# Linear attention: the second query round and the last value copies moved across the copy of the turned key maxima

## The chip, the cores and the metric

The kernel runs on one core of a Trainium2 chip. The metric is the device time of one execution in microseconds, as the median of three runs. The engines are named as in the profile: PE (TensorE), DVE (VectorE), ACT (ScalarE), POOL (GpSimd) and SP (the DMA queue used here). Each engine takes its own instructions in order; engines wait for each other through semaphores.

## What is computed

The program is a chain of seven layers on an input of 32 images of 32 channels and 16 x 16 pixels: a group norm and a linear attention, a convolution with a shared 51 x 51 kernel, a linear transformer, a mixture of experts, a squared attention and routed blocks. The change touches only the first layer, whose reference is, cut to what matters:

```
qkv = einsum('bchw,oc->bohw', xn, w_qkv)      # xn: x scaled to unit norm over channels
q, k, v = split(qkv, 3, axis=1)               # 4 heads of 32 channels, n = 256 pixels
k = concatenate([mk, k], axis=-1)             # 4 memory columns ahead of the pixels
v = concatenate([mv, v], axis=-1)
q = softmax(q, axis=-2) * scale               # over the 32 channels of a head
k = softmax(k, axis=-1)                       # over the pixels
context = einsum('bhdn,bhen->bhde', k, v)
out = einsum('bhde,bhdn->bhen', context, q)
return einsum('bchw,oc->bohw', out, w_out) + b_out
```

## The kernel before

The images lie on the partitions in four groups of 32 channels (J = 4), and the pixels of eight images per group are cut into 16 units of 128 tokens. `linear_attention` projects them in four rounds of four units for each of queries, keys and values. A query round takes PSUM banks 0 to 3, a value round and a key round take banks 4 to 7. Each engine's order is written out by hand; nothing is scheduled by a planner, and the only freedom that an engine has is to wait.

What each engine does in the stretch that the change touches:

- PE: query_round(0), value_round(2), value_round(3); then a transpose of the key maxima in parts (L484, into bank 4), a transpose of the memory exponentials (L487, bank 5) and a small memory product (L490, bank 6), each waiting for what the engine ahead copied; then key_round(0), query_round(1), key_round(1), key_round(2), query_round(2), key_round(3) and the context products (L456), between which the turned queries (L445) and query_round(3) stand. A query round waits until the units of the round ahead have been subtracted (they share the banks), a key round until ACT has taken the exponentials of the key round ahead.
- DVE: for every unit a `subtract_maxima` (L573 the maximum of each head, L575 the subtraction out of PSUM into SBUF) and an `invert_sums` (L581 the sum of the exponentials, L583 its reciprocal). In round 0, behind unit 2, it copies the turned key maxima (L599), the turned memory exponentials (L601) and the memory product (L603) out of PSUM. Behind the last unit of a round stand the four `invert_sums` of that round.
- ACT: four value copies for each value round (L646: four banks, 512 columns a unit), the factors of the memory terms (L668), then query exponentials (L657) and pairs of key exponentials (L651) in a fixed order: queries 0 to 3, keys 0, keys 1, queries 4 to 6, keys 2, query 7, keys 3, query 8, and then query exponentials between copies of the turned queries (L661).
- POOL: key maxima in three parts, the memory terms (they wait for L603 on DVE), and for every unit the product of the exponentials with their inverted sums (L760).

The transpose of the key maxima writes bank 4, which the last value round has filled, so it waits until all value units are copied. The copy L599 gives the rows that open each key product, so key_round(0) waits for it and for L603.

Of the kernel before, what the change touches and what calls it, by code (L numbers as in the profile page):

```python
# [9 lines left out]
ACT = mybir.ActivationFunctionType  # L10
# [3 lines left out]
B, C, H, W = 32, 32, 16, 16  # L14
# [5 lines left out]
NCH = COLS // CH  # L20
QN = 4
NQ = N // QN
HEADS, DH = 4, 32
# [247 lines left out]
def linear_attention(nc, m, sem, d):  # L271

    ps = m.ps
    UN = G * S
    RND = 4
# [29 lines left out]
    memterm = sem("la_memterm")  # L305
    v_ready = sem("la_v_ready")
    v_copied = sem("la_v_copied")
    k_ready = sem("la_k_ready")
    kexp_done = sem("la_kexp_done")
    q_ready = sem("la_q_ready")  # L310
# [48 lines left out]
    def qf_unit(u):  # L359

        g, s = divmod(u, S)
        return qf[:, :, :].rearrange("p (j g) n -> p j g n", j=J)[:, :, g, s * 128:(s + 1) * 128]

    def turned_queries(u):
        return ps[:, 7 - u % 2, :].rearrange("p (j n) -> p j n", j=J)
# [7 lines left out]
    with nc.Block() as block:  # L373
        @block.tensor
        def _(pe):
# [26 lines left out]
            def value_round(r):  # L402

                if r:
                    pe.wait_ge(v_copied, RND * r)
                for i in range(RND):
                    for j in range(J):
                        mm = pe.matmul(ps[:, 4 + j, i * 128:(i + 1) * 128], xn[rows_of(j), tokens(RND * r + i)],
                                       m.wvo[rows_of(j), :], start=True, stop=True)
                mm.then_inc(v_ready, 1)  # L410
# [16 lines left out]
            def query_round(r):  # L427

                if r:
                    pe.wait_ge(qsub_done, RND * r)  # L430
                for i in range(RND):
                    for j in range(J):
                        mm = pe.matmul(ps[:, j, i * 128:(i + 1) * 128], xn[rows_of(j), tokens(RND * r + i)],
                                       m.wqkv[rows_of(j), 0:128], start=True, stop=True)
                mm.then_inc(q_ready, 1)
# [26 lines left out]
            def key_maxima_round(r):  # L462

                for i in range(J):
# [14 lines left out]
            query_round(0)  # L479
            value_round(2)  # L480
            value_round(3)
            pe.wait_ge(parts, 4)
            pe.wait_ge(v_copied, UN)
            pe.transpose(ps[:, 4, 0:64].bitcast(BF16), m.kparts[:, :, :].rearrange("p j r -> p (j r)"),  # L484
                         m.identb[:, :]).then_inc(turned, 1)
            pe.wait_ge(memexp_done, 1)
# [6 lines left out]
            pe.wait_ge(turned_copied, 1)  # L493
            pe.wait_ge(w2mem_copied, 1)
            key_round(0)
            query_round(1)
            key_round(1)
            key_round(2)
            query_round(2)
# [27 lines left out]
        def _(dve):  # L527
            own = sem("la_dve")
            for g in range(G):
                c = slice(g * N, (g + 1) * N)  # L530
# [3 lines left out]
            for g in range(BY_ACT, G):  # L534
                c = slice(g * N, (g + 1) * N)
# [53 lines left out]
                                  m.kmem[:, b0:b1, :], ALU.add).then_inc(w2_summed, 1)  # L589

            for r in range(NCH):
                dve.wait_ge(q_ready, r + 1)
                for i in range(RND):
                    subtract_maxima(RND * r + i)
                    if r == NCH - 1 and i:
                        invert_sums(RND * r + i - 1)
                    if r == 0 and i == 2:
                        dve.wait_ge(turned, 1)
                        dve.tensor_copy(m.kmrow[:, :], ps[:, 4, 0:64].bitcast(BF16)).then_inc(turned_copied, 1)  # L599
                        dve.wait_ge(mem_ready, 1)  # L600
                        dve.tensor_copy(m.kemt[:, :], ps[0:MEM, 5, 0:128]).then_inc(mem_copied, 1)  # L601
                        dve.wait_ge(w2mem_ready, 1)
                        dve.tensor_copy(m.w2mem[:, :], ps[:, 6, 0:33]).then_inc(w2mem_copied, 1)  # L603
                    if r == 2 and i == 2:
                        dve.wait_ge(memterm, 2)
                        sum_context(0)
                for i in range(RND if r < NCH - 1 else 0):
                    invert_sums(RND * r + i)
# [24 lines left out]
        @block.scalar  # L633
        def _(act):
            for g in range(BY_ACT):
                c = slice(g * N, (g + 1) * N)
                act.activation(m.tmpB[:, c], m.x[:, c], ACT.Square, bias=m.shift8[:, g:g + 1],
                               scale=m.inv8[:, g:g + 1]).then_inc(squared, 1)
            act.wait_ge(norm2_ready, 1)
            act.activation(m.rstd[:, NQ:2 * NQ], ps[:, 4, 0:NQ], ACT.Sqrt).then_inc(norm_ready, 1)  # L640
            act.wait_ge(memmax_ready, 1)
            act.activation(m.kem[:, :], m.memk[:, :], ACT.Exp, bias=m.small[:, 1:2]).then_inc(memexp_done, 1)

            def copy_values(u):
                i = u % RND
                act.activation(m.vtok1[u][:, :, :, 0:C],  # L646
                               ps[:, 4:8, i * 128:(i + 1) * 128].rearrange("p j (h c) -> p j h c", h=HEADS),
                               ACT.Copy).then_inc(v_copied, 1)

            def key_exponentials(r, a):  # L650
                act.activation(ek[:, RND * r:RND * (r + 1), 2 * a:2 * a + 2, :].rearrange("p u j d -> p j u d"),  # L651
                               ps[:, 4 + 2 * a:6 + 2 * a, :].rearrange("p j (u d) -> p j u d", u=RND),
                               ACT.Exp).then_inc(kexp_done, 1)

            def query_exponentials(u):
                act.wait_ge(qsub_done, u + 1)
                act.activation(qt[:, u, :, :], qt[:, u, :, :], ACT.Exp).then_inc(qexp_done, 1)  # L657

            def copy_queries(u):
                act.wait_ge(qt_ready, u + 1)  # L660
                act.activation(qf_unit(u), turned_queries(u), ACT.Copy).then_inc(qt_copied, 1)  # L661

            for r in range(NCH):
                act.wait_ge(v_ready, r + 1)
                for i in range(RND):
                    copy_values(RND * r + i)
            act.wait_ge(km_ready, 1)
            act.activation(m.kfac[:, :], m.kmax[:, :], ACT.Exp, bias=m.small[:, 0:1], scale=-1.0).then_inc(f_done, 1)  # L668
            def key_round(r):
                act.wait_ge(k_ready, r + 1)  # L670
                for a in range(2):
                    key_exponentials(r, a)

            for u in range(RND):
                query_exponentials(u)
            key_round(0)
            key_round(1)
            for u in (4, 5, 6):
                query_exponentials(u)
            key_round(2)  # L680
            query_exponentials(7)
            key_round(3)
            query_exponentials(8)
            copy_queries(0)
            query_exponentials(9)
            query_exponentials(10)
            copy_queries(1)
            query_exponentials(11)
            copy_queries(2)
            for i in range(4):  # L690
                query_exponentials(12 + i)
                copy_queries(3 + i)
            for u in range(7, UN):
                if u not in BY_V:
                    copy_queries(u)
# [2270 lines left out]
```

## Time and profile before

| what | before |
|---|---|
| median of three runs | 572.55 us (572.53 to 574.28) |
| profiled execution | 572.74 us |
| its span, first to last instruction | 570.9 us |
| mean granted TensorE clock | 0.956 of full speed |
| PE busy | 503.4 us, 88% of the span |
| DVE busy | 409.6 us, 72% |
| ACT busy | 311.7 us, 55% |
| POOL busy | 158.4 us, 28% |

The profile is one execution. Times in it are in microseconds from the start of the span, durations of single instructions in nanoseconds. 1.84 us lie outside the span. An engine's busy time does not say whether it is waited for: the timeline shows each instruction with its start, its duration and, in brackets, the idle time ahead of it with the instruction that ended it. The linear attention runs from about 10 to 86 us of the span.

### The profile page before, as it was taken

To read this page: it belongs to the slowest core of one execution; us is meant where nothing else is said; L and a number is where in the kernel's file an instruction comes from. 1 tells how busy PE (TensorE), PEld (TensorE's weight loads), DVE (VectorE), ACT (ScalarE), POOL (GpSimd) and SP (SyncE) were. 2 spreads that over 40 slices of the span, in tenths; PEclk is the share of its full clock that TensorE was granted. 3 is DMA by queue.
4 is the path that set the end of the run, shared out by engine and by line. 5 is a ranking of instruction groups with operands and counts; after the bars stand their busy time and mean duration, and the time that the engine had idled before them with its cause. 6 is when DMAs were issued, how large, how long until landed. Compare 5 with 4: busy or idle time off the path is not lost. (4 is left out here: it accounts for less than half of the span.)

```text
span 570.9 us, 15184 instructions
## 1 busy us (share of the span) xinstructions
PE 503.4 (88%) x6313; PEld 293.7 (51%) x6313; DVE 409.6 (72%) x751; ACT 311.7 (55%) x543; POOL 158.4 (28%) x210
## 2 busy tenths in 40 slices
PE   8957778999888889989888878989999999999993
PEld 3547654466665553255555544444664566366520
DVE  5758978686444589967788857975786776777664
ACT  3255635243344310267988875355776577667573
POOL 0106423000000000043565640000692078038600
PEclk9976899999999879999999999979999999999998
DMA  8400007000000075000000000000000000000002
GB/s 262 47 6 3 3 2 242 1 2 1 2 1 2 1 175 121 0 3 1 2 1 2 3 20 2 0 8 13 1 3 6 8 2 1 12 2 2 1 7 77
DMA packets 22560, 15.02 MB, mean 26 GB/s; under 512 B 17466, under 2 KB 20570, under 8 KB 22363
## 3 DMA queue, kind: packets, MB, share of 16 engines
q1 hardware_dynamic: 22490, 14.00, 9.8%
q8 instruction: 55, 0.90, 0.6%
q14 instruction: 15, 0.11, 0.1%
HBM read 8.71 MB, written 1.08 MB: 17 GB/s over the span
## 5 line engine op out<-in xcount | busy, mean ns | idle before, releaser
L2327 DVE TENSOR_REDUCE R<-ps 128x4 f32<-128x1024 f32 x48 | 56.6, 1221 | 21.3 <-PE ps L1849 20.9
L2150 ACT ACTIVATE R<-ps 128x512 f32<-128x512 f32 x96 | 52.0, 597 | 11.0 <-PE ps L1861 10.9
L2233 POOL TENSOR_TENSOR R<-R 128x512 f32<-128x512 f32 x42 | 53.3, 1270 | 16.4 <-ACT R L2150 16.4
L1609 POOL TENSOR_TENSOR R<-R 128x512 f32<-128x512 f32 x32 | 45.4, 1417 | 39.8 <-DVE R L1542 39.8
L1542 DVE TENSOR_TENSOR R<-ps,lasting 128x512 f32<-128x512 f32 x64 | 41.1, 685 | 11.7 <-PE ps L1464 11.7
L1861 PE MATMUL ps<-tmpA,R 32*128 32x256 f32 x384 | 48.3, 378 | 0.0
L1576 ACT ACTIVATE R<-R 128x1536 f32<-128x1536 f32 x32 | 47.3, 1479 | 0.1
L1849 PE MATMUL ps<-R,tmpA 32*128 32x256 f32 x384 | 45.4, 392 | 0.0
L1464 PE MATMUL ps<-R,Q 32*128 32x128 f32 (+1 forms) x512 | 29.9, 346 | 10.0 <-ACT R L1592 10.0
L1861 PEld LDWEIGHTS ps<-tmpA,R 32*128 32x128 f32 x384 | 36.5, 185 | 0.5
L1464 PEld LDWEIGHTS ps<-R,Q 32*128 32x128 f32 x512 | 23.9, 184 | 20.8 <-DVE R L1542 16.9
L2008 PE MATMUL ps<-R,early 32*128 32x512 f32 x160 | 31.2, 713 | 1.2 <-DVE R L166 1.2
L1849 PEld LDWEIGHTS ps<-R,tmpA 32*128 32x128 f32 x384 | 29.6, 184 | 4.0 <-ACT tmpA L2124 2.3
L2217 POOL TENSOR_TENSOR R<-R 128x8 f32<-128x8 f32 x24 | 4.9, 206 | 94.9 <-DVE R L2327 94.9
L2173 ACT ACTIVATE R<-ps,b 128x1024 f32<-128x1024 f32 x25 | 26.8, 1113 | 7.1 <-PE ps L2008 7.1
L1592 ACT ACTIVATE R<-ps 128x256 f32<-128x256 f32 x64 | 24.2, 381 | 10.1 <-DVE R L1542 10.1
L101 PE MATMUL ps<-lasting 128*128 128x512 f32 x54 | 28.9, 664 | 0.6 <-DVE R L1124 0.6
L1492 PE MATMUL ps<-R 128*32 128x128 f32 (+1 forms) x512 | 27.2, 332 | 2.1 <-ACT R L1576 2.1
L2390 DVE TENSOR_SCALAR R<-ps,b 128x1024 f32<-128x1024 f32 x15 | 19.3, 1284 | 9.8 <-PE ps L2008 9.1
L1910 PE MATMUL ps<-R,Q 128*32 128x256 f32 x384 | 25.6, 384 | 0.0
L2062 PE MATMUL ps<-R,early 128*32 128x512 f32 x160 | 22.4, 631 | 1.2 <-DVE R L2390 1.2
L1108 DVE COPY R<-ps 32x256 f32<-32x256 f32 (+2 forms) x30 | 14.0, 477 | 11.5 <-PE ps L1042 3.9
(336 smaller groups left out, 1103.9 us busy)
## 6 DMA issues: line engine op xcount, KB each, us to landing
R<-z SPq DMA_DIRECT2D x32, 128.0 KB, 2.4
R<-in_qv SPq DMA_DIRECT2D x1, 2560.0 KB
x<-in_x SPq DMA_DIRECT2D x4, 256.0 KB, 3.5
out<-x SPq DMA_DIRECT2D x4, 256.0 KB, 2.6
lasting<-in_lasting SPq DMA_DIRECT2D x1, 811.0 KB, 8.4
early<-in_early SPq DMA_DIRECT2D x1, 793.5 KB, 7.0
scatter<-in_scatter SPq DMA_DIRECT2D x1, 512.0 KB, 5.4
P<-scratch_w SPq DMA_DIRECT2D x16, 32.0 KB, 2.6
```

The source lines that it names most:

```text
L101: pe.matmul(m.ps[:, bank, :], t[:, 0:128], t[:, 0:CH], start=True, stop=True)
L1464: mm = pe.matmul(ps[:, 2 * (u % 3) + k, s * N:N + s * 128], k_[rows, at:at + 128], m.qm[rows, h, at:(g + 1) * N], start=True, stop=True)
L1492: mm = pe.matmul(ps[rows_of(j), 6 + g % 2, s * 128:N], vm[:, (2 * g + s) * J + j, h, :], m.att[:, u % SLOTS, k, at:at + N - s * 128], star ...
L1542: dve.tensor_tensor(diagonal(u), ps[:, 2 * (u % 3):2 * (u % 3) + 2, :] .rearrange("p k (d n) -> p k d n", n=128)[:, :, 0:3:2, :], m.causal ...
L1576: act.activation(a, a, ACT.Silu, scale=1.0 / AHD).then_inc(act_done, 1)
L1609: pool.tensor_tensor(diagonal(u), diagonal(u), diagonal(u), ALU.mult).then_inc(diag_squared[1], 1)
L1849: return pe.matmul(ps[:, j, half * N:(half + 1) * N], ut[rows_of(j), at:at + 128], h[rows_of(j), cols], start=True, stop=True)
L1861: mm = pe.matmul(ps[:, turned_bank(g, j), t * N:(t + 1) * N], h[rows_of(j), at:at + 128], ut[rows_of(j), g * N:(g + 1) * N], start=False, ...
L2008: mm = pe.matmul(ps[:, 2 * (r % 3) + i, :], m.w1[p][rows_of(j), :], h[rows_of(j), k * CH:(k + 1) * CH], start=True, stop=True)
L2150: act.activation(m.et[:, g % 2, j, :], ps[:, turned_bank(g, j), :], ACT.Exp)\
L2233: pool.tensor_tensor(m.esum[:, g % 2, two, :], m.et[:, g % 2, two, 0:N], m.et[:, g % 2, two, N:2 * N], ALU.add).then_inc(sg["halves_added" ...
L2327: dve.tensor_reduce(m.parts[:, g % 2, :, a:a + 2, 3 * g].rearrange("p s i -> p i s"), ps[:, a:a + 2, :].rearrange("p i (s m) -> p i s m", ...
```

## The change

Three things move or are split.

- query_round(1) stands on PE right behind value_round(3), ahead of the transpose of the key maxima, instead of behind key_round(0).
- The four value copies of the last round are split by banks: ACT copies banks 4 and 5 of each unit (256 columns), DVE banks 6 and 7 (another 256). The transpose of the key maxima waits for both, through a second semaphore.
- On DVE the three copies of the turned parts stand behind unit 3 instead of unit 2 of round 0, and around them: the four value copies and the subtraction of unit 4 ahead, the subtractions of units 5, 6 and 7 behind. The four sums of round 0 come behind those, and round 1 of the loop is left with its sums alone.

```diff
--- before.py
+++ after.py
@@ -305,6 +305,7 @@
     memterm = sem("la_memterm")
     v_ready = sem("la_v_ready")
     v_copied = sem("la_v_copied")
+    v_copied_v = sem("la_v_copied_v")
     k_ready = sem("la_k_ready")
     kexp_done = sem("la_kexp_done")
     q_ready = sem("la_q_ready")
@@ -360,6 +361,13 @@
 
         g, s = divmod(u, S)
         return qf[:, :, :].rearrange("p (j g) n -> p j g n", j=J)[:, :, g, s * 128:(s + 1) * 128]
+
+    def value_unit(u, j0):
+        return m.vtok1[u][:, j0:j0 + 2, :, 0:C]
+
+    def value_banks(u, j0):
+        i = u % RND
+        return ps[:, 4 + j0:6 + j0, i * 128:(i + 1) * 128].rearrange("p j (h c) -> p j h c", h=HEADS)
 
     def turned_queries(u):
         return ps[:, 7 - u % 2, :].rearrange("p (j n) -> p j n", j=J)
@@ -479,8 +487,10 @@
             query_round(0)
             value_round(2)
             value_round(3)
+            query_round(1)
             pe.wait_ge(parts, 4)
             pe.wait_ge(v_copied, UN)
+            pe.wait_ge(v_copied_v, RND)
             pe.transpose(ps[:, 4, 0:64].bitcast(BF16), m.kparts[:, :, :].rearrange("p j r -> p (j r)"),
                          m.identb[:, :]).then_inc(turned, 1)
             pe.wait_ge(memexp_done, 1)
@@ -493,7 +503,6 @@
             pe.wait_ge(turned_copied, 1)
             pe.wait_ge(w2mem_copied, 1)
             key_round(0)
-            query_round(1)
             key_round(1)
             key_round(2)
             query_round(2)
@@ -589,18 +598,27 @@
                                   m.kmem[:, b0:b1, :], ALU.add).then_inc(w2_summed, 1)
 
             for r in range(NCH):
-                dve.wait_ge(q_ready, r + 1)
+                if r != 1:
+                    dve.wait_ge(q_ready, r + 1)
                 for i in range(RND):
-                    subtract_maxima(RND * r + i)
+                    if r != 1:
+                        subtract_maxima(RND * r + i)
                     if r == NCH - 1 and i:
                         invert_sums(RND * r + i - 1)
-                    if r == 0 and i == 2:
+                    if r == 0 and i == RND - 1:
+                        for u in range(UN - RND, UN):
+                            dve.wait_ge(v_ready, NCH)
+                            dve.tensor_copy(value_unit(u, 2), value_banks(u, 2)).then_inc(v_copied_v, 1)
+                        dve.wait_ge(q_ready, 2)
+                        subtract_maxima(RND)
                         dve.wait_ge(turned, 1)
                         dve.tensor_copy(m.kmrow[:, :], ps[:, 4, 0:64].bitcast(BF16)).then_inc(turned_copied, 1)
                         dve.wait_ge(mem_ready, 1)
                         dve.tensor_copy(m.kemt[:, :], ps[0:MEM, 5, 0:128]).then_inc(mem_copied, 1)
                         dve.wait_ge(w2mem_ready, 1)
                         dve.tensor_copy(m.w2mem[:, :], ps[:, 6, 0:33]).then_inc(w2mem_copied, 1)
+                        for u in range(RND + 1, 2 * RND):
+                            subtract_maxima(u)
                     if r == 2 and i == 2:
                         dve.wait_ge(memterm, 2)
                         sum_context(0)
@@ -660,10 +678,13 @@
                 act.wait_ge(qt_ready, u + 1)
                 act.activation(qf_unit(u), turned_queries(u), ACT.Copy).then_inc(qt_copied, 1)
 
-            for r in range(NCH):
+            for r in range(NCH - 1):
                 act.wait_ge(v_ready, r + 1)
                 for i in range(RND):
                     copy_values(RND * r + i)
+            act.wait_ge(v_ready, NCH)
+            for u in range(UN - RND, UN):
+                act.activation(value_unit(u, 0), value_banks(u, 0), ACT.Copy).then_inc(v_copied, 1)
             act.wait_ge(km_ready, 1)
             act.activation(m.kfac[:, :], m.kmax[:, :], ACT.Exp, bias=m.small[:, 0:1], scale=-1.0).then_inc(f_done, 1)
             def key_round(r):
```

On PE, from query_round(0) to the first key products of the stretch: L433 is a query round, L408 two value rounds, L484, L487 and L490 the turned parts, L420 and L423 the products of a key round. Before:

```order
L433 MATMUL ps<-early,tmpA 128x128 x16
L408 MATMUL ps<-P,tmpA 128x128 x32
L484 MATMUL ps<-identb,P 128x128
L487 MATMUL ps<-lasting,P 4x128
L490 MATMUL ps<-P 32x33 x4
L420 MATMUL ps<-P 128x128 x4
```

And now, with the new line numbers:

```order
L441 MATMUL ps<-early,tmpA 128x128 x16
L416 MATMUL ps<-P,tmpA 128x128 x32
L441 MATMUL ps<-early,tmpA 128x128 x16
L494 MATMUL ps<-identb,P 128x128
L497 MATMUL ps<-lasting,P 4x128
L500 MATMUL ps<-P 32x33 x4
L428 MATMUL ps<-P 128x128 x4
```

A second query round has come in between the value rounds and the transposes; its old place behind the first key round is empty.

On DVE, from the subtraction of unit 2 on: L573 and L575 are a unit's maximum and subtraction, L599, L601 and L603 the copies of the turned parts, L581 and L583 a sum and its reciprocal. Before:

```order
L573 TENSOR_REDUCE z<-ps 128x16
L575 TENSOR_TENSOR R<-ps,z 128x512
L599 COPY P<-ps 128x128
L601 COPY P<-ps 4x128
L603 COPY P<-ps 128x33
L573 TENSOR_REDUCE z<-ps 128x16
L575 TENSOR_TENSOR R<-ps,z 128x512
L581 TENSOR_REDUCE z<-R 128x16
```

And now, from the subtraction of unit 3 on:

```order
L582 TENSOR_REDUCE z<-ps 128x16
L584 TENSOR_TENSOR R<-ps,z 128x512
L611 COPY R<-ps 128x8x32 x3
L611 COPY P<-ps 128x8x32
L582 TENSOR_REDUCE z<-ps 128x16
L584 TENSOR_TENSOR R<-ps,z 128x512
L615 COPY P<-ps 128x128
L617 COPY P<-ps 4x128
L619 COPY P<-ps 128x33
```

Ahead of the copies of the turned parts stand now the subtraction of unit 3, four value copies and the subtraction of unit 4; behind them three more units and only then the sums.

## Rows read from the trace of the kernel before

**Rows 1.** Stretches, length, busy PE, PEld, DVE, ACT, POOL (instructions), granted clock, DMA.

```profile
36.50:38.50 2.00, 2.00 (x32) 1.72 (x32) 0.09 (x1) 0.00 (x0) 0.00 (x0) 0.50 0.00 0
38.60:42.30 3.70, 0.81 (x10) 0.31 (x10) 0.75 (x4) 3.70 (x8) 0.00 (x0) 0.50 0.02 4
42.40:46.40 4.00, 4.00 (x77) 3.86 (x80) 3.86 (x9) 1.84 (x3) 4.00 (x4) 0.50 0.01 2
46.60:49.80 3.20, 1.63 (x54) 1.33 (x48) 3.10 (x7) 1.56 (x3) 1.98 (x2) 1.00 0.02 5
50.80:55.30 4.50, 4.42 (x80) 3.94 (x80) 3.78 (x9) 3.17 (x5) 2.17 (x3) 0.50 0.01 2
...
60.20:63.40 3.20, 3.20 (x84) 2.47 (x84) 3.10 (x8) 1.63 (x3) 0.02 (x1) 0.50 0.02 5
63.60:68.80 5.20, 5.17 (x260) 4.32 (x249) 5.03 (x11) 3.01 (x6) 3.84 (x4) 1.00 0.02 3
56.10:74.90 18.80, 14.52 (x611) 11.90 (x611) 18.22 (x36) 10.36 (x18) 8.55 (x10) 0.89 0.02 4
```

**Rows 2.** Timeline, value round to key round: start, us, engine, line; idle in brackets.

```profile
33.25 0.69 DVE L575 TENSOR_TENSOR R<-ps,z 128x512 f32<-128x512 f32 x1
...
34.57 0.69 DVE L575 TENSOR_TENSOR R<-ps,z 128x512 f32<-128x512 f32 x1
...
36.42 2.09 PE L408 MATMUL ps<-P,tmpA 32*128 32x128 f32 x32 [2.19 <-ACT R L646]
...
38.58 1.57 ACT L646 ACTIVATE R<-ps 128x512 f32<-128x512 f32 x3 [2.21 <-PE ps L408]
...
40.03 0.62 ACT L646 ACTIVATE P<-ps 128x512 f32<-128x512 f32 x1
...
40.79 0.26 PE L484 MATMUL ps<-identb,P 128*128 128x128 bf16 x1 [2.28 <-ACT P L646]
...
41.09 0.23 DVE L599 COPY P<-ps 128x128 bf16<-128x128 bf16 x1 [4.50 <-PE ps L484]
...
42.38 0.29 PE L420 MATMUL ps<-P 32*128 32x128 bf16 x4 [0.41 <-DVE P L603]
```

**Rows 3.** Groups by line and form, copies out of PSUM: busy us, mean ns.

```profile
L1108 DVE COPY R<-ps 32x256 f32<-32x256 f32 x18 | 7.7, 426 | 4.3 <-PE ps L1042 3.9
...
L613 DVE COPY R<-ps 128x512 f32<-128x512 f32 x3 | 2.1, 687 | 2.6 <-PE ps L445 2.6
...
L910 ACT ACTIVATE R<-ps 128x256 f32<-128x256 f32 x8 | 3.1, 386 | 11.4 <-PE ps L877 11.4
```

**Rows 4.** Timeline of the key rounds, up to the copies of turned queries.

```profile
44.90 1.81 PE L433 MATMUL ps<-early,tmpA 32*128 32x128 f32 x32
...
45.19 1.94 ACT L651 ACTIVATE R<-ps 128x1024 f32<-128x1024 f32 x2 [0.97 <-PE ps L423]
...
47.19 0.23 PE L420 MATMUL ps<-P 32*128 32x128 bf16 x4 [0.47 <-ACT R L651]
...
48.77 1.94 ACT L651 ACTIVATE R<-ps 128x1024 f32<-128x1024 f32 x2 [1.64 <-PE ps L423]
...
53.30 1.92 PE L433 MATMUL ps<-early,tmpA 32*128 32x128 f32 x32
...
53.59 1.94 ACT L651 ACTIVATE R<-ps 128x1024 f32<-128x1024 f32 x2 [1.33 <-PE ps L423]
...
56.08 0.69 DVE L581 TENSOR_REDUCE z<-R 128x16 f32<-128x512 f32 x1 [1.36 <-ACT R L657]
...
57.69 1.94 ACT L651 ACTIVATE R<-ps 128x1024 f32<-128x1024 f32 x2 [1.64 <-PE ps L423]
...
59.77 0.24 PE L456 MATMUL ps<-R 128*32 128x33 f32 x5 [2.17 <-ACT R L651]
...
77.68 0.69 DVE L613 COPY R<-ps 128x512 f32<-128x512 f32 x1 [1.77 <-PE ps L445]
```

**Rows 5.** Busy time by stretch, a later stage.

```profile
340.10:343.30 3.20, 3.20 (x5) 1.22 (x4) 0.00 (x0) 1.11 (x2) 0.14 (x1) 0.50 0.31 84
```

## The prediction

> **What bounds the kernel now.** I read the page's slices first: ahead of 60 us no engine is full for long and the granted TensorE clock dips below one, so this stage is bound by hand-overs and not by one engine. Then I read the timeline from the last value round to the first context products, and last the busy times by stretch, for the clock. Two things are to be seen.
>
> First, a hand-over around 38 to 42 us. The last value round ends on PE at 36.42 + 2.09 = 38.51; ACT copies its four units from 38.58 to 40.65; only then may PE transpose the key maxima (40.79), DVE copy them (41.09) and, behind it, the memory terms, and PE begin key_round(0) at 42.38 [rows 2]. DVE stands for 4.50 us in front of the copy at 41.09 [rows 2].
>
> Second, a ring behind it: key_round(r) on PE writes four banks, ACT takes their exponentials, and only then may key_round(r+1) write the same banks. ACT's four pairs of exponentials start at 45.19, 48.77, 53.59 and 57.69, and the first context product stands at 59.77 [rows 4]. The steps are 3.58, 4.82, 4.10 and 2.08 us, and each is PE's round, then ACT's 1.94. The step of 3.58 has its key round at a granted clock of 1.00 (2.4 GHz), the step of 4.82 at 0.50 (1.2 GHz) [rows 1]: 1.24 us is what a key round costs more at the low level. query_round(1), which the change takes out of this ring, runs at 44.90 to 46.71, under ACT's 45.19 to 47.13 [rows 4]: it costs the ring nothing. DVE is nearly full after that, but its own start there hangs on the ring: at 56.08 it has waited 1.36 us for ACT, which issues query exponential 7 behind the third pair of key exponentials [rows 4].
>
> **The change, part by part.**
>
> Query round 1 behind the last value round. It waits for the subtraction of unit 3, now also ahead on DVE: a unit takes 1.32 us from start to start (33.25 to 34.57) [rows 2], so the third ends at 33.25 + 2 x 1.32 + 0.69 = 36.6 and unit 3 at 37.9, before the value round does. No wait. The round costs PE 1.81 to 1.92 us at the low level [rows 4], overlapping the tail of what is ahead of it by 0.2, so it ends near 40.2, and the transpose queued behind it can start there.
>
> Value copies on two engines. Four copies of 256 columns on ACT cost at most 4 x 0.386 = 1.54 us, end by 40.1. The trace has no DVE copy of 128 x 256; the nearest are 32 x 256 at 0.426 us and half of a 512-column one at 0.687 [rows 3]: four lie between 4 x 0.34 = 1.37 and 4 x 0.43 = 1.70. I take 1.6, nearer to the row with the same column count; from 38.58 they end at 40.2 (39.95 to 40.3), against 40.65 before. So the transpose stands at about 40.3 instead of 40.79: 0.5 us earlier. No work on DVE hides the four copies, but they lie in its 4.50 us wait.
>
> The subtraction of unit 4 in front of the copy of the key maxima. DVE is in order, and this pair waits for query round 1 (40.2) and takes 1.32 us. The transposed maxima are ready at 40.6 and lie there: DVE gets to them at about 41.6 instead of 41.09. Queued behind that pair are the two memory copies, PE's memory product, all key rounds, and POOL's memory terms. The chain from the copy to key_round(0), 41.09 to 42.38, keeps its 1.29 us. So key_round(0) starts near 42.9: **+0.5 us**. The bounds are +0.35 (copies at 1.37 and the query round at its overlap) and +0.7 (query round without overlap, 40.4).
>
> Subtractions 5 to 7 move ahead of the sums of round 0. ACT waited for unit 3 ahead of its fourth query exponential and no longer does, but that lies inside its wait for key_round(0): nothing. DVE's work behind the hand-over is two subtractions shorter, 2.64 us, and starts 0.5 later, so it is 2.1 us ahead at the end of round 1. The wait of 1.36 us at 56.08 only grows by that, because query exponential 7 stays queued on ACT behind the third pair of key exponentials: nothing. POOL's normalising of units 0 to 3 starts about 3 us later, since DVE's sums of round 0 now stand behind subtractions 5 to 7 instead of one; it is 4 us of work [rows 1] and its first taker stands behind 59.77 [rows 4]: nothing.
>
> The clock. Before, the rise to 1.00 came at the end of 4 us in which PE was full, key_round(0) and query_round(1) back to back (42.40 to 46.40 busy 4.00, granted 0.50), and key_round(1) then ran at 1.00 (46.60 to 49.80) [rows 1]. The change takes query_round(1) out of that place: behind key_round(0) PE stands for ACT's 1.94 us. The last value round alone, 2 us full at 0.50 with idle time on both sides [rows 1], brought no rise. So I take key_round(1) to run at 0.50: **+1.24 us**. On the other side value_round(3) and query_round(1) are now 3.8 us back to back, ending at 40.2, and may bring the rise there; but then PE has only two transposes and the small memory product until 42.9, about 0.8 us of work (0.81 in 38.60 to 42.30) [rows 1], and each wait of 2 us in this stretch was followed by 0.50. I take key_round(0) at 0.50, as before.
>
> By the Trainium skill, "TensorE: Matmul & The Clock Gate", Part 1, the default state is throttled and sustained activity releases it, so the new back-to-back pair would release the clock ahead of key_round(0), and the sum would be the second rival's -0.7 instead of +0.9. The trace agrees that a full stretch brings the release (1.00 in the row of 46.60, behind 4.00 us full), and shows no release that outlasted a wait of this length.
>
> The third and fourth key round. key_round(2) ran at 0.50 before [rows 1] and would after. key_round(3) comes behind key_round(2) and query_round(2), back to back as before, and took 4.10 - 2.0 = 2.1 us, between the two levels (1.58 and 2.81); starting 1.7 later it meets the clock already risen: -0.5. So the pair 2 of exponentials, and with it DVE's wait, ends 0.5 + 1.24 = 1.74 later, and the first context product 1.74 - 0.5 = **1.24 later**.
>
> From there PE is full: 3.20 of 3.20 us at 0.50, then 5.17 of 5.20 at 1.00 [rows 1]. If the clock rises at the same moment as before, near 63.5, half of the delay is given back, since it falls in work at half speed: +0.6 is left. If it rises the same time after the first product, 1.24 is left. I take the middle, +0.9, that is 0.35 given back. DVE, 1.7 late and 18.22 of 18.80 us busy there [rows 1], has a wait of 1.77 us behind it, at 77.68 [rows 4], that takes this up.
>
> **Sum.** +0.5 + 1.24 - 0.5 - 0.35 = +0.9 us. The profiled execution took 572.74 us (span 570.9 and 1.84 around it), the median is 572.55, 0.2 below. 572.55 + 0.9 gives **573.4 us**, +0.15%.
>
> **The rivals.** A measurement of this kernel can tell about 0.3% from no change, 1.7 us: below 570.8 is faster, above 574.3 slower.
>
> DVE sets the end. For it: DVE is the fullest engine from 56.1 to 74.9. Then the 2.1 us that it is ahead come off: 570.4, faster. Against: its wait of 1.36 us on ACT at 56.08. It decides only if ACT reaches query exponential 7 earlier.
>
> The clock rises before key_round(0) and holds. Then that round takes 1.58 instead of 2.81 us, and key_round(1) stays at 1.00: +0.5 - 1.23 = -0.7, so 571.8, no change that can be told. For it: 3.8 us back to back ahead of 40.2. Against: the 2.5 us of nearly idle PE behind it.
>
> The clock stays at 0.50 longer. query_round(1) no longer fills the gap in the ring, and the pair of key_round(2) and query_round(2) comes too late for key_round(3): key_round(1) +1.24, key_round(3) 0.7 instead of -0.5, and the context products run another 3.3 us at 0.50 as in the stretch 60.20 to 63.40, half of which is lost: 0.5 + 1.24 + 0.7 + 1.6 = +4.0, so 576.5, **slower**. It decides if the granted clock is still 0.50 when key_round(3) starts. For it: before, that rise fell inside key_round(3), by its 2.1 us, so it came late. Against: the pair is as long as the one that brought the rise between 46.40 and 46.60 [rows 1].
>
> A later stage is met at another moment by the clock. The stretch at 340.1 to 343.3 is full at 0.50 [rows 5]; one such stretch of 3.2 us fewer or more is 1.6 us: 571.8 or 575.0 with my sum.
>
> **Chances.** Forecast 0.50, clock held high 0.14, DVE sets the end 0.12, clock low for longer 0.18, a later stage 0.06 (0.04 of it slower). Faster: 0.12. Slower: 0.18 + 0.04 = 0.22. No change: 0.50 + 0.14 + 0.02 = 0.66. The likeliest case alone reaches from 573.1 (+0.35 for +0.5, half of the delay given back) to 574.0 (+0.7 for +0.5, nothing given back). The range goes from 571.0 (the held clock with +0.35 for +0.5, and reaching halfway into key_round(2), -0.6) to 575.9: the slow rival begins at 575.0, where the context products lose nothing further, and ends at 576.5, and its upper part, 0.08, is left out, as is DVE's case, 0.12.
>
> **What would show it.** Right: key_round(0) 0.35 to 0.7 later than 42.38; a subtraction between the value copies and the copy of the key maxima; DVE waiting over 3 us for ACT ahead of the sums of unit 7; ACT's second pair of key exponentials 4.8 instead of 3.58 behind the first; granted clock 0.50 in key_round(1). Wrong: a granted clock of 1.00 in key_round(0) or (1), a DVE copy of 256 columns above 0.5 us, or a DVE that no longer waits on ACT ahead of round 2.

## The result and the profile after

The changed kernel took 577.72 us (median of 5 runs, 575.25 to 578.53) against 572.55 us for the kernel before (5 runs, 571.29 to 574.28): a ratio of 1.0079, 95% interval 1.0045 to 1.0113. It was **slower by 5.2 us** where 573.4 was forecast, and it lay outside the range. A later comparison of 12 runs each gave 2.1 us. Means in this document are over all runs; without the slow ones, those over 1.5% above the fastest of their kernel, that comparison gives 2.4 us. So two questions stand: what the change costs, and why five runs showed more than twice that.

The page of the profiled execution after (575.25 us, the shortest of its five; the four longer runs left no trace): span, slices of the granted clock, busy time of each engine.

```profile
span 573.5 us, 15181 instructions
...
PE 504.4 (88%) x6306; PEld 298.7 (52%) x6313; DVE 411.5 (72%) x755; ACT 310.7 (54%) x543; POOL 158.6 (28%) x210
...
PEclk9765899999999969999999999989999999999998
```

The span grew by 2.6 us. The row of the granted clock before:

```profile
PEclk9976899999999879999999999979999999999998
```

Its first slices read 9, 9, 7, 6, 8 (14 us each); now 9, 7, 6, 5, 8. Part of that loss stands ahead of everything that the change moves. Stretches of after, with the columns of [rows 1]:

```profile
16.90:20.20 3.30, 1.89 (x49) 1.50 (x50) 2.48 (x4) 0.00 (x0) 0.00 (x0) 1.00 0.25 31
20.30:37.20 16.90, 16.80 (x132) 12.14 (x124) 10.81 (x19) 3.33 (x7) 0.98 (x4) 0.50 0.34 33
37.40:40.70 3.30, 1.30 (x33) 0.98 (x32) 3.06 (x5) 2.01 (x5) 0.00 (x0) 1.00 0.00 0
40.80:61.10 20.30, 13.74 (x242) 11.96 (x246) 15.03 (x33) 10.32 (x19) 8.34 (x9) 0.50 0.01 2
61.30:80.00 18.70, 13.61 (x636) 11.19 (x632) 16.70 (x33) 11.17 (x19) 7.96 (x8) 1.00 0.02 5
```

From 20.3 to 37.2 us PE is full at 0.50, in instructions that the change doesn't touch. Before, that time was at 1.00 up to 36:

```profile
20.30:35.90 15.60, 12.83 (x164) 7.93 (x156) 13.71 (x25) 5.73 (x12) 0.98 (x4) 1.00 0.38 35
```

So the last value round starts at 41.41 instead of 36.42 [rows 2], **+4.99 us before the change begins**. The last row but one of the five after is the stage of the change: one stretch of 0.50 through the hand-over and three key rounds, where before it was broken by 46.60 to 49.80 at 1.00 [rows 1].

Timeline of after, last value round to first key round: start, us, engine, line, operation, idle before it and what ended it.

```profile
41.41 2.09 PE L416 MATMUL ps<-P,tmpA 32*128 32x128 f32 x32 [2.18 <-ACT R L664]
...
43.28 1.93 PE L441 MATMUL ps<-early,tmpA 32*128 32x128 f32 x32
43.57 0.94 ACT L687 ACTIVATE R<-ps 128x256 f32<-128x256 f32 x3 [2.21 <-PE ps L416]
43.57 1.09 DVE L611 COPY R<-ps 128x256 f32<-128x256 f32 x3 [0.62 <-PE ps L416]
...
44.58 0.41 DVE L611 COPY P<-ps 128x256 f32<-128x256 f32 x1
...
45.14 0.29 PE L494 MATMUL ps<-identb,P 128*128 128x128 bf16 x1
...
45.28 0.69 DVE L582 TENSOR_REDUCE z<-ps 128x16 f32<-128x512 f32 x1 [0.29 <-PE ps L441]
46.00 0.69 DVE L584 TENSOR_TENSOR R<-ps,z 128x512 f32<-128x512 f32 x1
46.61 0.21 DVE L615 COPY P<-ps 128x128 bf16<-128x128 bf16 x1
...
47.80 0.30 PE L428 MATMUL ps<-P 32*128 32x128 bf16 x4 [0.40 <-DVE P L619]
```

The four DVE copies run from 43.57 to 44.99, 1.42 us, and the query round ends at about the same time (43.28 + 1.93). The transpose stands at 45.14, 1.57 us behind the first copy; DVE waits 0.29 us for the query round ahead of unit 4. The unit's maximum and subtraction (45.28, 46.00) stand on DVE in front of the copy at 46.61, as the prediction said. The value round starts 4.99 later than before and key_round(0) 5.42 later: the hand-over cost 0.43.

The ring behind it, same view, up to the first context product:

```profile
50.62 1.94 ACT L669 ACTIVATE R<-ps 128x1024 f32<-128x1024 f32 x2 [3.56 <-PE ps L431]
...
52.61 0.29 PE L428 MATMUL ps<-P 32*128 32x128 bf16 x4 [2.06 <-ACT R L669]
...
55.44 1.94 ACT L669 ACTIVATE R<-ps 128x1024 f32<-128x1024 f32 x2 [2.88 <-PE ps L431]
...
57.92 0.69 DVE L590 TENSOR_REDUCE z<-R 128x16 f32<-128x512 f32 x1 [2.92 <-ACT R L675]
...
60.26 1.94 ACT L669 ACTIVATE R<-ps 128x1024 f32<-128x1024 f32 x2 [1.33 <-PE ps L431]
...
62.75 0.69 DVE L590 TENSOR_REDUCE z<-R 128x16 f32<-128x512 f32 x1 [2.18 <-ACT R L675]
...
63.84 1.94 ACT L669 ACTIVATE R<-ps 128x1024 f32<-128x1024 f32 x2 [1.12 <-PE ps L431]
...
65.92 0.24 PE L464 MATMUL ps<-R 128*32 128x33 f32 x5 [2.15 <-ACT R L669]
```

The steps between the pairs are 4.82, 4.82 and 3.58 us, where [rows 4] gave 3.58, 4.82 and 4.10. PE stands 2.06 us for ACT ahead of key_round(1), and that round runs at 0.50: +1.24. key_round(3) runs at 1.00: -0.52. DVE's wait for ACT ahead of sums went from 1.36 to 2.92 and 2.18 us. The context products start 1.16 later than before, counted from the value round, and the first output product 0.55 later. Before and after:

```profile
81.42 3.66 PE L522 MATMUL ps<-R,P 128*32 128x256 f32 x64
...
86.96 3.66 PE L531 MATMUL ps<-R,P 128*32 128x256 f32 x64
```

The rest of the span, 489.5 us before, is 486.5 now: two late stretches at 0.50 in the trace of before (the one of [rows 5], and one from 186.4 to 189.8) aren't in this one. Before, then after:

```profile
186.00:190.00 4.00, 3.78 (x10) 3.00 (x11) 0.96 (x3) 0.05 (x1) 0.00 (x0) 0.57 0.00 0
...
340.00:344.00 4.00, 4.00 (x6) 1.55 (x6) 0.68 (x2) 1.21 (x2) 0.24 (x1) 0.57 0.25 68
...
186.00:190.00 4.00, 3.00 (x60) 2.47 (x52) 0.85 (x2) 0.75 (x2) 0.00 (x0) 1.00 0.02 4
...
340.00:344.00 4.00, 1.86 (x44) 0.87 (x36) 1.40 (x3) 3.15 (x4) 1.42 (x1) 1.00 0.01 2
```

The instructions of after stand about 5.5 us later, but there too, between 61.5 and 204 us and between 215 and 382, no stretch is at 0.50. So 4.99 + 0.55 - 2.9 = 2.6. The two large terms lie in code that didn't change.

### The profile page after: what moved, and what is told of

It reads as the page before. It is cut to its first block and busy times, and to the rows that moved or that the text cites. A ratio compares the mean times of both kernels' runs of the same rounds, so it can differ in the third digit from the quotient of the medians.

```text
span 573.5 us, 15181 instructions
## 1 busy us (share of the span) xinstructions
PE 504.4 (88%) x6306; PEld 298.7 (52%) x6313; DVE 411.5 (72%) x755; ACT 310.7 (54%) x543; POOL 158.6 (28%) x210
## 3 DMA queue, kind: packets, MB, share of 16 engines
HBM read 8.71 MB, written 1.08 MB: 17 GB/s over the span
```

## The experiments

Theory A: the change costs what its steps add (about 1 to 2 us), and the rest is the clock at other places, by chance of the execution. Theory B: the changed program draws the early low clock itself, and costs about 5. Rivals within A: the unit on DVE ahead of the turned maxima costs it, or the missing query round in the ring does. Means below are over all runs of a kernel, with a standard error.

**Both kernels again, and each part alone.** after_again and before_again have no edit. split_only is the kernel before with the value copies shared by two engines; sub4_late is the changed kernel with unit 4 behind the copies of the turned parts:

```
 split_only:  query_round(1) stays behind key_round(0); DVE copies its half of the four value units behind unit 2
 sub4_late:
-    dve.wait_ge(q_ready, 2)
-    subtract_maxima(RND)
     dve.wait_ge(turned, 1)
...
-    for u in range(RND + 1, 2 * RND):
+    dve.wait_ge(q_ready, 2)
+    for u in range(RND, 2 * RND):
```

> The kernel before once more, nothing altered, as a measure of how far the same program moves between executions. Theory A: its trace, too, can show a granted clock of 0.50 between 20 and 37 us, and its runs spread over 571 to 577 us. Theory B: value_round(3) begins at 36.4 again and all runs lie in 571 to 574.5 us, ratio 1.000 within 0.003.

> The changed kernel once more, nothing altered. In its first trace value_round(3) began at 41.41 us instead of 36.42, 5.0 us late ahead of every moved instruction, with a granted clock of 0.50 from 20 to 37 us; from there to the output products (81.42 before, 86.96 after) only 0.55 us more were lost. Theory A, the early loss is a state that the clock fell into in that execution and not the change's: in another execution the granted clock stays at 1.00 there, value_round(3) begins at 36.4 and the time is 573 to 574 us. Theory B, the early loss comes with this program: value_round(3) begins near 41.4 again and the time is 575 to 578 us.

> The kernel before with the last value copies split between ACT and DVE and nothing moved: query_round(1) stays behind key_round(0), the copies of the turned parts stay behind unit 2. From value_round(3) to key_round(0) 5.4 us instead of 5.96, the pair of exponentials 1 still 3.6 us behind pair 0 since query_round(1) keeps PE full between them. Theory A: 572.0 us, 0.5 below before. Theory B, any new shape of this stage costs the early clock: 575 us or more, with value_round(3) late as in the changed kernel.

> The changed kernel with the subtraction of unit 4 behind the three copies of the turned parts instead of ahead of them. By the forecast's step on that subtraction, the copy of the key maxima no longer lies behind 1.32 us of DVE work: from the start of value_round(3) to key_round(0) 5.3 us instead of 6.39 in the changed kernel and 5.96 before; key_round(1) still at a granted clock of 0.50 (4.8 us behind the first pair of key exponentials). Time 1.1 us below the changed kernel under theory A and B alike. If that subtraction is not the hand-over's price, 6.4 us and the same time as the changed kernel.

Measured, 12 runs each: before_again 573.27 ± 0.73 (568.10 to 576.97), after_again 575.33 ± 0.72, split_only 572.88 ± 0.83, sub4_late 574.06 ± 0.88. The unaltered kernel beside them, 35 runs, gave 573.8 with a spread from 566.99 to 579.66. The ratio of after_again is 1.0035 (0.9995 to 1.0074). So 13 us lie between executions of one program, and the change costs about 2, which this comparison alone doesn't tell from nothing. Theory B, that only the changed program draws the early low clock, falls by before_again's own stretches, in the columns of [rows 1]:

```profile
24.50:27.80 3.30, 3.30 (x38) 2.87 (x41) 2.27 (x4) 0.00 (x0) 0.00 (x0) 0.50 0.64 59
27.90:31.20 3.30, 2.86 (x18) 1.12 (x12) 2.63 (x5) 2.06 (x4) 0.00 (x0) 1.00 0.49 48
31.30:34.60 3.30, 3.30 (x45) 2.87 (x46) 2.48 (x5) 0.00 (x0) 0.31 (x2) 0.50 0.00 0
...
41.60:58.50 16.90, 11.56 (x206) 10.04 (x210) 12.96 (x27) 10.53 (x17) 8.19 (x8) 0.50 0.01 2
```

The kernel before, too, can run at 0.50 ahead of the stage; here its last value round starts at 40.29. This doesn't show that it does so as often as the changed one. Its key_round(1) ran at 0.50 as well, with query_round(1) in the ring, as the first two pairs of its exponentials show:

```profile
48.15 1.94 ACT L651 ACTIVATE R<-ps 128x1024 f32<-128x1024 f32 x2 [0.97 <-PE ps L423]
...
52.96 1.94 ACT L651 ACTIVATE R<-ps 128x1024 f32<-128x1024 f32 x2 [2.88 <-PE ps L423]
```

The step is 4.81 us here and 3.58 in [rows 4]: the clock in the ring of the kernel before isn't the same in each execution.

**The stage alone.** To take the later chances away, four kernels end behind linear attention: the six later layers are left out, and idle matmuls at the start of the stage are six instead of two, meant to hold the early clock.

```
-    turn_over(pe, 2)
+    turn_over(pe, 6)
...
-    peripheral_convolution(nc, m, sem, d)
...
-    routed_blocks(nc, m, sem)
+    (m.x is stored to the output)
```

> The kernel before, ended behind the linear attention: the six later layers are left out and the residual sum is stored. Four more idle matmuls stand on PE ahead of the first key maxima, at 18.5 us, so that PE is fuller there. Without the later layers a difference of 1 us is no longer lost in the spread of their own clock states (567 to 580 us for the unaltered kernel before). Some 92 us; value_round(3) begins at 36.8 in most executions, and from the end of value_round(3) to key_round(0) 3.87 us as in both traces of the kernel before.

> The changed kernel, cut and filled the same way (later layers left out). Theory A, the change costs what its own stage loses and the rest of the first 5 us was chance: 0.5 to 1.2 us above cut_before in the median, 4.3 us from the end of value_round(3) to key_round(0), the pair of key exponentials 1 4.8 us behind pair 0. Theory B, the program brings a low clock ahead of the change: 4 to 5 us above cut_before, with value_round(3) late. Theory C, no cost at all: within 0.3 us.

> split_only (value copies on two engines, nothing moved), cut and filled the same way (later layers left out). Its first trace had 3.22 us from the end of value_round(3) to key_round(0) against 3.87. Theory A: 0.6 us below cut_before. If the clock's states weigh more than the hand-over: no difference to cut_before beyond 0.3 us.

> sub4_late (query_round(1) early, the subtraction of unit 4 behind the copies of the turned parts), cut and filled the same way (later layers left out). The hand-over is 1.2 us shorter than in cut_after. By the forecast's steps: 1.1 us below cut_after; against cut_before 0.7 us earlier at key_round(0), but key_round(1) has lost query_round(1) as its lead and runs at 0.50 (+1.24, half of it given back): between 0.5 below and 0.5 above cut_before.

Measured, 6 runs each: 92.00 ± 0.46, 93.98 ± 0.35, 92.72 ± 0.67 and 93.21 ± 0.64. Two of them once more, the cut kernels again:

> cut_before once more (later layers left out), beside cut_after_2 on one chip, since six runs each leave the difference of 2.0 us uncertain by 1. Expected 92.0 within 0.8; the step from the pair of exponentials 0 to pair 1 below 4.5 us.

> cut_after once more (later layers left out). Theory A: 1.0 to 2.5 us above cut_before_2, the step from pair 0 to pair 1 at 4.8 us. If the first difference was chance of the executions: within 0.7 us of cut_before_2.

92.88 ± 0.64 (6 runs) and 94.11 ± 0.59 (7). Together, cut_after 94.05 against cut_before 92.44: **+1.6 ± 0.5 us**. The order of the parts is that of the full kernels (shared copies alone +0.3, unit 4 late +0.8, all +1.6), but the steps between them are no larger than their errors; cut_split, expected 0.6 us below cut_before, isn't below it. The ring of cut_after, exponentials, DVE's sums and the stretch:

```profile
46.28 1.94 ACT L669 ACTIVATE R<-ps 128x1024 f32<-128x1024 f32 x2 [4.12 <-PE ps L431]
...
51.10 1.94 ACT L669 ACTIVATE R<-ps 128x1024 f32<-128x1024 f32 x2 [2.88 <-PE ps L431]
...
53.59 0.69 DVE L590 TENSOR_REDUCE z<-R 128x16 f32<-128x512 f32 x1 [2.92 <-ACT R L675]
...
38.10:58.40 20.30, 13.82 (x242) 11.41 (x239) 13.52 (x30) 11.37 (x19) 9.27 (x9) 0.50 0.01 2
```

and of cut_before, its first two pairs and the stretches around the rise:

```profile
45.26 1.94 ACT L651 ACTIVATE R<-ps 128x1024 f32<-128x1024 f32 x2 [0.97 <-PE ps L423]
...
49.16 1.94 ACT L651 ACTIVATE R<-ps 128x1024 f32<-128x1024 f32 x2 [1.96 <-PE ps L423]
...
37.80:47.90 10.10, 6.72 (x122) 5.48 (x122) 6.08 (x15) 6.39 (x11) 5.45 (x6) 0.50 0.01 2
48.10:51.30 3.20, 1.13 (x44) 0.92 (x44) 3.13 (x6) 2.14 (x3) 0.55 (x1) 1.00 0.02 5
```

With the query round in the ring the rise comes at 48, inside key_round(1) (step 3.90); without it the level stays 0.50 to 58.4 (step 4.82). In after, PE stood 2.06 us ahead of that round. The wait alone doesn't set the level: in cut_sub4 PE stood 2.06 us ahead of key_round(1) as well, and the round began at 1.00 (45.60 us; the level fell near 46.8).

**The idle matmuls by themselves.** The full kernels with six idle matmuls, and the cut ones with two, as in the original (six later layers left out):

> The whole kernel before with four more idle matmuls on PE at 18.5 us, ahead of the first key maxima. value_round(3) begins at 36.7 to 37.2 in its trace. If the early fall of the clock costs something in the mean, 1 to 2 us below the kernel before (median 572 against 573 to 574); if not, the same within 0.5 us, or 0.3 slower for the added matmuls.

> The whole changed kernel with the same four idle matmuls. Theory A: 1.5 to 2 us above filled_before, with value_round(3) at 36.7 to 37.2. Theory B: the fill takes the early loss away and leaves 0.5 us. In the stage: key_round(0) 4.0 to 4.3 us behind the end of value_round(3) and key_round(1) at a granted clock of 0.50.

> The kernel before, ended behind the linear attention (the six later layers left out), without the four added idle matmuls. If the granted clock falls at some 20 to 37 us in some executions of any program, its runs spread further than cut_before's (89.9 to 93.1): up to 97, median 92 to 94. If the kernel before never falls there: the same 92.0 and the same spread as cut_before.

> The changed kernel cut the same way (later layers left out), without the added idle matmuls. Theory A (the early fall is chance, common to both programs): 1.5 to 2.0 us above cut_before_nofill, as cut_after stood 1.6 to 2.0 above cut_before. Theory B (the program brings the early fall): 4 to 6 us above cut_before_nofill, 97 us and more in nearly all runs.

Full: 572.72 ± 0.68 and 574.95 ± 0.65 (12 runs each), +2.2. Cut: 92.99 ± 0.83 (6) and 94.97 ± 0.81 (7), +2.0. Within these errors the change costs the same with the fillers and without them. The fillers themselves gain 0.4 to 0.9 us, less than the errors, and don't always keep the early clock up: in cut_after_2 a stretch at 0.50 lay ahead of them (14 to 18 us) and the last value round started at 39.02; in cut_before_gapfill below, the level was 0.50 as they ran (19.2 to 22.6 us) and the round started at 40.24.

**Is it the ring?** If the alternation of PE and ACT sets the time, splitting it should free it. Each key round is written in two halves, each half behind its own exponential (cut kernels, six later layers left out):

```
-    if r:
-        pe.wait_ge(kexp_done, 2 * r)
+    for a in range(2):
+        if r:
+            pe.wait_ge(kexp_done, 2 * r - 1 + a)
...
-    act.wait_ge(k_ready, r + 1)
+        act.wait_ge(k_ready, 2 * r + a + 1)
```

> cut_before (later layers left out, four idle matmuls added) with each key round in two halves: banks 4 and 5 are written as soon as ACT has taken the first of the two exponentials of the round ahead, banks 6 and 7 after the second, and ACT starts on a half as soon as it is written. If the alternation of PE and ACT sets the time of this stretch, the step from one pair of exponentials to the next falls from 3.6 to 4.8 us to about 3, and the kernel gains 1 to 3 us on cut_before (92.0). If DVE sets it, the steps shrink and the time stays within 0.5 us.

> cut_after with the same halves. Ring theory: the changed kernel's DVE is 2.1 us ahead and only waits for ACT's query exponentials behind the key rounds, so with a shorter ring the loss against the kernel before shrinks or turns: from 1 us below to 0.5 above cut_before_halves, and below cut_after (94.0) by 2 to 4 us. Rival, the lateness of the hand-over sets the time and not the ring: still 1.5 to 2 us above cut_before_halves.

Measured: 93.84 ± 0.77 (7 runs, median 92.61) and 93.15 ± 0.36 (6, median 93.35). With halves the means differ by -0.7 ± 0.85 instead of +1.6 ± 0.5. But the medians differ by +0.7: three of the seven runs of cut_before_halves, at 94.9 to 96.5, make its mean. So the runs hint at the ring and don't decide between it and the hand-over. Neither kernel is better than cut_before, from which cut_before_halves was expected to gain 1 to 3 us. cut_after_halves, second half of key_round(1) and DVE's sums:

```profile
50.47 1.02 ACT L670 ACTIVATE R<-ps 128x1024 f32<-128x1024 f32 x1 [0.74 <-PE ps L432]
...
52.05 0.69 DVE L591 TENSOR_REDUCE z<-R 128x16 f32<-128x512 f32 x1 [1.57 <-ACT R L676]
...
55.91 0.69 DVE L591 TENSOR_REDUCE z<-R 128x16 f32<-128x512 f32 x1 [1.23 <-ACT R L676]
```

ACT waits 1.08 us for the first half of that round and 0.74 for the second, together 1.82 instead of 2.88, and DVE 1.57 and 1.23 instead of 2.92 and 2.18.

**Filling the gap.** Two idle matmuls ahead of key rounds 1 to 3, as soon as ACT's first exponential frees the first half of the banks (six later layers left out):

```
+    pe.wait_ge(kexp_done, 2 * r - 1)
+    for _ in range(2):
+        pe.matmul(ps[:, 4, :], idle[:, 0:128], idle[:, 0:CH], start=True, stop=True)
```

> cut_before (later layers left out, four idle matmuls ahead of the key maxima) with two more idle matmuls ahead of key rounds 1, 2 and 3, into bank 4, as soon as ACT has taken the first of the two exponentials that read it; they stand in time in which PE waits for the second. If the level at which key rounds run is what the changed kernel loses, the steps between the pairs of exponentials fall towards 3.6 us here too (they were 3.6, 4.8 and 4.1 in the first trace) and the time falls by 0.5 to 2 us below cut_before (92.4 over 12 runs). If the clock does not matter there: 92.4 or up to 0.5 more for the added work.

> cut_after with the same idle matmuls between the key rounds (later layers left out). Ring theory: the step from the pair of exponentials 0 to pair 1 falls from 4.8 towards 3.6 us, since PE no longer stands there, and the time falls by 1 to 2 us below cut_after (94.05 over 13 runs), to within 0.8 us of cut_before_gapfill. If the hand-over alone is the loss: steps and difference stay, 1.6 us above cut_before_gapfill.

92.93 ± 0.60 (7 runs) and 94.12 ± 0.45 (6). In cut_after_gapfill the fillers shortened the wait to 1.53 us and key_round(1) still ran at the low level: its steps are 4.87, 4.87 and 3.58.

```profile
46.33 0.63 PE L424 MATMUL ps<-scatter 128*128 128x512 bf16 x1 [1.53 <-ACT R L676]
```

So the run doesn't show what a higher clock there would give the changed kernel; in it the fillers did not bring the level back. The trace of cut_before_gapfill has all three steps at 3.58 us, but so has that of cut_before_2, without fillers: the two reach the first context product 15.63 us behind key_round(0), where the other five traces of the kernel before took 17.0 to 18.1. The time of cut_before_gapfill isn't below that of cut_before.

## Why the prediction was wrong

**Where the traces agree.** Twelve traces stand side by side, six of the kernel before (whole, cut, with idle matmuls or without) and six of the changed one.

| | before, mean (range) | after, mean (range) | change | forecast |
|---|---|---|---|---|
| last value round's first copy to key_round(0), us | 3.80 (3.80) | 4.18 (3.82 to 4.80) | +0.38 | +0.5 |
| first to second pair of key exponentials | 3.93 (3.58 to 4.81) | 4.82 (4.81 to 4.82) | +0.89 | +1.24 |
| key_round(0) to first context product | 17.13 (15.63 to 18.12) | 18.05 (17.75 to 18.38) | +0.92 | +0.74 |
| first context product to first output product | 21.78 (20.96 to 23.03) | 21.25 (21.01 to 21.79) | -0.53 | -0.35 |

*The hand-over.* Right in the sum. DVE's copies took 0.41 us each instead of the 0.40 assumed, and overlapped to 1.42 together. The two variants part the cost between the query round and unit 4. split_only's value copies, transpose, copy of the maxima and key_round(0):

```profile
39.30 1.09 DVE L609 COPY R<-ps 128x256 f32<-128x256 f32 x3 [1.07 <-PE ps L416]
...
40.87 0.26 PE L493 MATMUL ps<-identb,P 128*128 128x128 bf16 x1 [1.63 <-DVE P L609]
...
41.17 0.22 DVE L611 COPY P<-ps 128x128 bf16<-128x128 bf16 x1 [0.45 <-PE ps L493]
...
42.46 0.29 PE L428 MATMUL ps<-P 32*128 32x128 bf16 x4 [0.41 <-DVE P L615]
```

sub4_late's:

```profile
38.21 1.08 DVE L611 COPY R<-ps 128x256 f32<-128x256 f32 x3
...
40.37 0.29 PE L494 MATMUL ps<-identb,P 128*128 128x128 bf16 x1
...
40.70 0.22 DVE L613 COPY P<-ps 128x128 bf16<-128x128 bf16 x1 [1.07 <-PE ps L494]
...
41.99 0.29 PE L428 MATMUL ps<-P 32*128 32x128 bf16 x4 [0.41 <-DVE P L617]
```

From the copies' start to key_round(0): 3.16 with the copies shared and nothing else, 3.78 with the query round in front of the transpose, 4.23 in after with unit 4 in front of the copy as well (3.80 before, [rows 2]). So sharing the copies gains 0.64. What takes it back differs by trace. In after the transpose stands 1.57 us behind the first copy, as in split_only without a query round, so there the round didn't hold it; unit 4, which the round held up by 0.29, cost the rest. In sub4_late, with the query round at 0.50 (38.35 to 40.44), the transpose stands at 2.16: there the round cost 0.6. In cut_sub4, where the level rose to 1.00 in the query round, the whole is 2.95.

*The clock in the ring.* The mechanism held: in all six traces of the changed kernel key_round(1) ran at 0.50. What failed is that the term was taken against one trace of before: there too the level differs by execution (five of six steps at 3.58 to 4.15, one at 4.81), so against its mean the step costs 0.89, not 1.24. Nor is the early query round the whole cause: in the two traces with it early and unit 4 late the step was 4.82 and 3.76. The Trainium skill, "TensorE: Matmul & The Clock Gate", "A second HAM failure mode: psum-queue depth-cycling", tells of a kernel that cycles through PSUM banks with short idles between groups of matmuls and swings between the levels. The trace of after fits: 1.00 from 37.4 to 40.7, 0.50 to 61.1, then 1.00, in a stage in which PE stands 2.06 us between rounds; that the idles are the reason no run here shows.

*DVE's lead.* Right: it became waiting, 2.92 and 2.18 us where over 3 was named as the sign, and the rival in which DVE sets the end didn't occur. (The 4 us given for POOL's normalising is right, 4.07 in the trace of before, but the row that it names counts the memory terms too.)

*The rivals on the clock.* It did not rise ahead of key_round(0) in the first trace of the changed kernel. In after_again and filled_after it rose within the query round, as the second rival has it, but fell 0.3 to 0.4 us into key_round(0) (1.00 to 48.2 and 43.4 us), so key_round(1) was at 0.50 all the same. In cut_sub4 it rose and held to 46.8: key_round(0) took 1.58 us. So the argument against this rival, that no release in the trace of before outlasted such a wait, doesn't carry to every trace: in cut_sub4 the level outlasted one of 2.06 us. "The clock stays at 0.50 longer" would have shown a low key_round(3) and gave 576.5, near the measured time, but it isn't what happened: in after key_round(3) ran at 1.00 (step 3.58) and the context products did not run on at 0.50. The time came from elsewhere.

**The step that failed** is the one on the chances: "a measurement of this kernel can tell about 0.3%", and with it the rival "a later stage is met at another moment by the clock", with 1.6 us and 0.06. The prediction names no run for it; the three times that it had lay within 1.75 us. 107 runs of the kernel before, those in the first comparison among them, reach from 566.99 to 579.66 us (standard deviation 2.5). Code ahead of the change alone moves the start of the last value round: 36.0 to 40.3 us in the six traces of the kernel before, 37.0 to 41.9 in those of the changed one. No case of mine had a stage *ahead of* the change in it: the sum put that term at nothing, and in the trace of after it was +4.99 us. Means of five runs of each kernel then differ by chance by 1.6 us (2.5 x the root of 2/5), medians by more. The first comparison shows +5.2 in medians and +4.3 in means. All runs give 573.58 ± 0.24 for before and 575.87 ± 0.58 (17 runs) for after, **+2.3 ± 0.6 us** (0.4%); the pair with six idle matmuls gives +2.2 ± 0.9 and the cut pairs with whole key rounds +1.2 to +2.0.

**The size** is the second miss: +0.9 forecast, about +2 measured. The table's rows add to 0.38 + 0.92 - 0.53 = +0.77, with some 0.6 of uncertainty from six traces each. About 1 us between that and the runs isn't placed. The rows begin at the last value round; ahead of it, in code that is the same, these traces differ too: that round starts at 37.2 us in the mean before and 39.5 after, 2.3 ± 1.1 later. In the eight other traces it is the other way, 36.9 with query_round(1) early against 38.7 without. So whether the missing 1 us lies in the stage, ahead of it, or is a chance of so few traces stays open, and with it whether the changed program meets the early low clock more often.

**The sign:** the forecast direction inside the bound of 0.3% was slower, and it is slower, by 2.3 ± 0.6 us, not clear of that bound of 1.7. No variant beat the kernel before by more than its error: split_only (-0.4 ± 1.1 against before_again) is the nearest, having the gain of the hand-over without the loss in the ring; its cut form shows no gain (+0.3).

## What to carry to other kernels

A round of matmuls that hides under another engine may be what keeps TensorE full, and with it the clock up, for the next round: count the gap that it leaves, and that next round at the low level (4.82 us a step here instead of 3.58). A lead given to an engine that waits on another engine's fixed order is only more waiting there. Before a forecast of under 1%, ask for how far executions of the unchanged program differ; three close times don't tell, and where the spread is larger than the effect, cut the stage out, take many runs, and compare steps in several traces.

## What the runs showed of the hardware

The granted clock fell and rose at different instructions in executions of the same program: before_again was at 0.50 from 24.5 to 27.8 us and from 31.3 to 34.6, where the first trace of before shows 1.00, and 13 us lie between the shortest and the longest of the kernel before's 107 runs. I had read the level in a stretch as a property of the program. Two idle matmuls in a gap of 2 us didn't bring the high level back in the one trace of it (steps of 4.87 us against 4.82 without). A 128 x 256 copy out of PSUM took 0.41 us on DVE and 0.40 on ACT, each behind others on its engine.
